# The order of GpSimd's work in one iteration of the attention loop of a vision-transformer layer

## What is computed

```python
h = _L0_tok_ref(x, ...)                        # (16, 256, 192)
h = h + _L0_attn_ref(_layernorm(h), ...)       # first norm
h = h + _L0_ffn_ref(_layernorm(h), ...)        # second norm

# attention: 12 heads of 16, features of q and k
s = einsum('bhld,fd->bhlf', seq * d**-0.25, omega)
feat = F**-0.5 * (exp(s - sum(s)/2 - max(s)) + 1e-6)
a = qf @ cumsum(kf x v) / (qf . cumsum(kf) + 1e-6)
out = a @ w_out + b_out

# experts: logits = x @ gate_w + gate_b, the two best of 8,
# y_e = gelu(x @ w1[e] + b1[e]) @ w2[e] + b2[e], weighted sum,
# plus a small spectral branch over the 256 tokens of an image
```

## Time and profile before

| what | us |
|---|---|
| median of the runs | 953.88 |
| lowest, highest of the 3 runs | 946.09, 955.04 |
| the profiled execution, device time | 953.78 |
| its span in the trace | 952.1 |
| busy in the span: PE, PEld, DVE, ACT, POOL | 769.8, 721.4, 515.1, 442.0, 435.4 |
| mean granted clock of PE | 0.801 |

### The profile page before, as it was taken

The page is one execution under the profiler, slowest core; times in us unless marked ns, Lnnn a source line. Parts: engine busy times, 40 slices in busy tenths (PEclk is TensorE's granted clock), DMA queues, the critical chain, the costliest instruction groups (busy, mean ns, idle before and its releaser), DMA issues. The chain is left out here.

```text
span 952.1 us, 17124 instructions
## 1 busy us (share of the span) xinstructions
PE 769.8 (81%) x4943; PEld 721.4 (76%) x4944; DVE 515.1 (54%) x1472; ACT 442.0 (46%) x853; POOL 435.4 (46%) x457
## 2 busy tenths in 40 slices
PE   2871589888988898888887605999997999999960
PEld 1471479888988898888887605999997999999960
DVE  1640247455665555555553233788789765565520
ACT  1440365444444444444442003777775566666630
POOL 7741223233333322333332233677776676656532
PEclk9596589677787776777776555999999899999975
DMA  8903201111111011111100002243333244434327
GB/s 217 230 14 154 63 13 50 32 41 40 40 40 39 9 40 32 40 40 40 32 20 19 22 8 46 51 62 60 58 59 54 41 68 77 73 77 76 62 39 136
DMA packets 60016, 55.08 MB, mean 58 GB/s; under 512 B 24232, under 2 KB 51311, under 8 KB 59967
## 3 DMA queue, kind: packets, MB, share of 16 engines
q0 software_dynamic: 19840, 23.53, 14.7%
q1 hardware_dynamic: 35647, 27.76, 10.9%
q10 hardware_dynamic: 4480, 3.21, 1.0%
HBM read 32.52 MB, written 25.10 MB: 61 GB/s over the span
## 5 line engine op out<-in xcount | busy, mean ns | idle before, releaser
L1141 POOL DMA_INDIRECT result<-e_y,e_tag x78 | 138.7, 1779 | 96.0 <-DVE e_y L1471 84.2
L502 POOL DMA_INDIRECT tbl_dram<-a_entry,a_slot x64 | 63.1, 986 | 211.2 <-DVE a_entry L987 170.1
L1200 PE MATMUL e_yp<-x_w2s,e_hh 128*128 x468 | 142.3, 370 | 2.9 <-DVE e_y L1471 2.9
L585 PEld LDWEIGHTS a_ab<-a_values,a_masked 128*128 128x128 f32 x768 | 134.9, 262 | 10.0 <-issue 9.5
L585 PE MATMUL a_ab<-a_values,a_masked 128*128 (+1 forms) x768 | 138.8, 343 | 2.2 <-DVE a_masked L865 2.0
L1464 DVE TENSOR_TENSOR e_hl<-e_hid,e_hh 128x512 fp32r<-128x512 f32 x117 | 80.3, 691 | 92.0 <-ACT e_hh L1266 91.8
L1258 ACT ACTIVATE e_hid<-e_hidden,e_b 128x256 f32<-128x256 f32 x234 | 101.3, 474 | 56.2 <-PE e_hidden L1187 46.3
L1201 PE MATMUL e_yp<-x_w2s,e_hl 128*128 x468 | 118.8, 254 | 0.0
L1129 POOL DMA_INDIRECT e_x<-x_dram,e_tag x78 | 82.5, 1057 | 42.0 <-issue 22.5
L1266 ACT CAST e_hh<-e_hid 128x512 fp32r<-128x512 f32 x117 | 72.4, 621 | 61.8 <-PE e_yp L1201 61.8
L865 DVE TENSOR_TENSOR a_masked<-a_s,a_causal 128x512 f32<-128x512 f32 x96 | 65.6, 686 | 49.6 <-PE a_s L561 35.3
(11 more groups left out here) (252 smaller groups left out, 1691.9 us busy)
## 6 DMA issues: line engine op xcount, KB each, us to landing
a_raw<-in_ew SPq DMA_DIRECT2D x16, 288.0 KB, 3.0
t_hs<-in_ew SPq DMA_DIRECT2D x8, 384.0 KB, 9.7
t_hs<-in_ew SPq DMA_DIRECT2D x16, 192.0 KB, 10.9
h_dram<-t_hs SPq DMA_DIRECT2D x4, 768.0 KB, 4.2
a_hb<-h_dram SPq DMA_DIRECT2D x16, 192.0 KB, 2.4
result<-a_hb SPq DMA_DIRECT2D x16, 192.0 KB, 3.6
x_dram<-a_att SPq DMA_DIRECT2D x16, 192.0 KB, 2.0
spec_dram<-e_space ACTq DMA_DIRECT2D x16, 192.0 KB, 1.9
```

The source lines that it names most:

```text
L585: last = pe.matmul(beside(o + r * VW), masked[n % 2][:, r], own_and_zeros.unsqueeze(1).broadcast_to([P, 2, 2, VW]), start=n == 0 and r == ...
L1141: pool.indirect_dma_start(out=out, in_=y[:, j], in_offset=None, out_offset=bass.IndirectOffsetOnAxis(ap=tag[:, i % 8, j, 0:1].bitcast(U32) ...
L1200: pe.matmul(Y[:, j, 0:2 * D], hh[:, f, c], w(f, 2 * D), start=f == 0, stop=False, skip_group_check=True)
```

## The change

GpSimd's part of an iteration is put in another order: the second norm's root first, then `low_part(i, 0)`, the weights' low part, the first norm's root, `low_part(i, 1)`, and the four stores of the slot table last. No instruction is added or removed, and the waits go with their instructions. The other engines' code is the same.

```diff
             def emit(i, one, two, tail, choice):
+                if tail:
+                    rstd("rstd2_ready", i - 2, mv2, rstd2, "tail", 5 * (i - 2) + 4)
+                if one:
+                    low_part(i, 0)
+                    wait_apart(pool, s["high"], i + 1)
+                    v = lambda c: w2s[:, bass.ds(i, 1), :, c * D:(c + 1) * D].rearrange("k u f d -> k (u f) d")
+                    g.tensor_tensor(v(1), raw[:], v(0).bitcast(F32), ALU.subtract).then_inc(s["low"], 1)
+                    if not (fixed(i) and i == B - 1):
+                        rstd("rstd1_ready", i + 1, mv, rstd1, "norm_step", 5 * (i + 1) + 4)
+                    low_part(i, 1)
                 if choice:
                     if not fixed(i) or i >= 4:
                         pool.wait_ge(s["scattered"], 64 * (i - 3))
...
                             ).then_inc(s["scattered"], 16)
-                if tail:
-                    rstd("rstd2_ready", i - 2, mv2, rstd2, "tail", 5 * (i - 2) + 4)
-                if one:
-                    wait_apart(pool, s["high"], i + 1)
-                    v = lambda c: w2s[:, bass.ds(i, 1), :, c * D:(c + 1) * D].rearrange("k u f d -> k (u f) d")
-                    g.tensor_tensor(v(1), raw[:], v(0).bitcast(F32), ALU.subtract).then_inc(s["low"], 1)
-                    low_part(i, 0)
-                    if not (fixed(i) and i == B - 1):
-                        rstd("rstd1_ready", i + 1, mv, rstd1, "norm_step", 5 * (i + 1) + 4)
-                    low_part(i, 1)
```

## The result

| what | before | after |
|---|---|---|
| median of the runs, us | 954.4 | 841.8 |
| lowest, highest | 946.1, 955.0 | 834.9, 843.9 |
| the profiled execution: device time, span | 953.8, 952.1 | 842.2, 840.5 |
| mean granted clock of PE | 0.801 | 0.884 |

The ratio is 0.881 (95% interval 0.875 to 0.888). Forecast were 838 us, 822 to 880. On chip 3, where I ran the changed kernel once more, the ratio is 0.897 (0.892 to 0.903). On chip 14 it is 0.961 (0.950 to 0.972), with 928.7 us: a good part of the gain isn't there, for a reason that the prediction doesn't have. The experiments come to it.

The account below looks back on a forecast made before the run. PE bounds the loop, and the slow iterations' extra nine microseconds are mostly clock. 953.8 us, less 112.0 for iterations 3 to 15, less 4.0 at the pipeline's end, plus 0.5 for iteration 0, gives 838 us; range 822 to 880.

Parts of the forecast that it names:

- What bounds the kernel: Loop bound by PE; the nine microseconds between iterations of 27.02 and 17.88 us are mostly PE's lower clock.
- (1), the root: Second norm's root moved ahead of the stores: PE's gap of 2.54 us gone in each iteration 3 to 15.
- (2), the weights' low part: Moved behind the first low parts, no longer meeting the second norm's L827: cost nothing, bounds 0 and 1.39 us.
- The term for iteration 0: In iteration 0, where the halves follow closely, the later weights' low part costs 0.5 us once.
- (3), the landing: Stores at the iteration's end: median landing 0.8 us late for the next `place`; iterations of 18.4 us, bounds 17.9 and 21.3.
- The mark that I had given: Sign that the stores' new place was forecast right: DVE's L980 is preceded by a wait under 1 us.
- (4), the clock: If PE's gap in the loop stays below a microsecond, its clock stays at 2.4 GHz; otherwise only 2.5 us saved.
- rival A: Stores land about 20.8 us after the add, iterations of 21.3 us: 38 us more, 876 us; chance 13%.
- rival B: Clock falls nonetheless, from a new gap or thin PE work: 917 us, or 878 in half the iterations; chance 18%.
- (5), the end: End of the pipeline, iterations 16 and 17: earlier root saves 4.0 us together, bounds 2 and 10.
- C: Slower than before: `place` waits longer for the stores than the old gap; about 997 us, chance 2%.
- D: Root isn't what holds DVE: L827 still starts late without stores ahead, time within 1%; chance 3%.

## Why the prediction was right, and where not

**What bounds the kernel.** Right. The loop was PE's, and nine tenths of the gain lie in it.

**(1), the root.** Right to the digit: 1.79 us behind the add, gaps of over 0.5 us at the transpose in two of the thirteen iterations (0.78 and 2.07), PE's wait for `a_att` 5.3 us in place of 30.8, 2.4 of it already in iteration 16 (I had set the line at 8). The run with the stores first shows that the root is the cause: with only the weights' low part moved the gap is still 1.87 us. That the stores have to leave the low parts' way too, which the prediction took as given, is an estimate only, as the one run with the root alone moved was on a chip where something else was in the way.

**(2), the weights' low part.** L827 takes 0.66 us, as forecast, and the place of this operation in the order is worth nothing (chip 3: 260.9 and 258.6). The term for iteration 0 was mis-sized. There the first norm's root waits behind it and begins at 118.01, 1.0 us later than before, and then a part of PE's work behind it ran at the low clock (its transposes at 126.59 took 1.06 us): the start is 2.7 us longer, of which 0.3 lie ahead of iteration 0, against my 0.5.

**(3), the landing.** In most iterations the last store begins 14.4 to 14.7 us behind the add, a little sooner than my 15.0. The mean agrees, 18.45 us for the twelve iterations against 18.4, but by another sum: luck. I had 17.9 us and half a microsecond for a landing that comes too late in each iteration. DVE's wait for it was 1.7 us on average, and PE felt it in two iterations of the loop, with 0.78 us in iteration 4 and 2.07 us in iteration 12, because what counts for PE is that wait less 1.78 us. What fills the 18.45 us is PE's own work: it is busy for (239.66 - 23.12) / 12 = 18.05 us of them, where it was 17.69 in iteration 2, which was my base. The 18.3 us from the earlier trace rows, which I had only laid beside the sum, was the better base. The mark that I had given was wrong as well, and against my own numbers: I wrote that the wait ahead of L980 should be under 1 us, while a landing at 18.2 us makes it 18.2 - 16.3 = 1.9 us. I had written down what is left of it behind the 1.08 us for which DVE idled in iteration 3.

**(4), the clock.** Here lies the rest: 12 iterations at 18.45 and one at 25.27 give 246.7 us, not 239.2. I had one landing time for all images, the median with the extremes as bounds, and put the longest into rival A as a case that holds in every iteration or in none. It is one image's, and it could have been read: the fourth store of image 8 has the 5.8 us in the trace of before too, and its landing there costs nothing. A long landing in one iteration is a gap in that iteration, and one of 2 us was a fall. So rival B happened in one iteration in thirteen (in two on chip 3), and rival A was its cause. The microsecond that step 4 gave the clock as a bound had nothing behind it but the 0.44 us of one gap and the 2.4 us and more of the others; the gaps measured since lie on both sides between 0.8 and 1.9 us.

**(5), the end.** 5.5 us against 4.0.

**The sum.** That the total is only 4 us off is luck in part: the loop gave 7.5 us less than forecast and the start 2.2 less, the end 1.5 more, and the experts, whose code nobody changed, 4.3 us.

**The rivals.** A and B as above. C didn't happen: no last landing came later than the bound of 26.5 us. D is refuted by iteration 9. What was missing is a rival in which the stores hold other engines. B had "a new gap of a microsecond or more opens where ... `take_state` waits", and on chip 14 the gap opens at the mask just ahead of it, for a reason that no row of before shows. The range, 822 to 880, doesn't hold 928.7. From the trace of before this couldn't be seen; that all rows came from one chip could.

**The store beside `a_xn`'s L827.** In iteration 8 L827 runs from 269.47 to 270.14 on top of the first store, which takes 1.06 us, and so it does at its old place, beside nothing of the kind. The L827 pair takes 1.35 us where it meets L490 and 0.66 where it meets nothing. The Trainium skill, "SBUF — State Buffer", section "Who interferes with whom", has DVE's `tensor_scalar` lock the ports that it shares with GpSimd and a DMA issued from GpSimd starve meanwhile; I had 847 us as the sum by it. The trace agrees with the lock, and the starving doesn't show here. The hold on chip 14 is no case of that rule either: it stops ACT as well, and the same section of the Trainium skill says that "PE and ACT never wait on anyone".

## What to carry to other kernels

When PE's clock is at stake, ask of a wait not how long it is in the mean but how long its longest case is and in which iteration; one gap of 2 us cost 7 us of clock here on top of itself, and no gap below 0.8 us cost any. Work that can go to either end of an iteration may be better off in two halves at both: it was the one order that was fast on the chips with the hold, on all three where it ran. And an order of work that gained 12% on one chip gained 4% on another, so a gain that rests on how engines meet wants more than one chip.

## What the runs showed of the hardware that I had not expected

- On chips 13 and 14, ACT and DVE are held while GpSimd issues four indirect stores in a row, with everything there that they wait for by the program. With the stores at the end of an iteration, DVE's mask 0 starts 0.9 to 1.2 us behind the end of the last store in each of the 39 iterations of three runs; with them behind the root it is mask 3, at 0.9 to 1.0 us in twelve of 13. With them at the end ACT waits for up to 3.9 us; on chip 14 it starts 0.9 to 1.0 us behind the last store in all but one of its long waits, on chip 13 in six of eleven already half a microsecond before that store ends. DVE still started three instructions between 254.04 and 254.69, so it isn't a stop from the first store on. What they lack isn't shown; the trace of chip 14 lists no fetch of instructions from 230 to 412 us.
- The same gap doesn't always have the same effect on the clock: 1.87 us in ten iterations, five falls; and of three shorter ones beside them (1.45 to 1.76 us) three.
- A store of 128 rows of two words takes 2.1 to 6.5 us to land in a loop whose DMA share is 0.12 to 0.17, and the longest is always the same image's fourth store, in each of the six traces that show landings (5.8, 5.3, 6.2, 6.5, 5.8 and 6.3 us). Whether its rows or its place in the sequence is the reason stays open.
